# Fifth passes over 64 rows, two at a time, in the layer part of a language model's tower

## The reference

```python
def _block(x, g, bt, Wi, bi, cw, cb, wd, bd_, wB, bB_, wC, bC_, wo, bo):
    h = _layernorm(x, g, bt)
    uv = h @ Wi.T + bi
    u, v = (uv[..., :D], uv[..., D:])
    uc = _dwconv_causal(u, cw, cb)
    delta = jax.nn.softplus(uc @ wd.T + bd_)
    Bm = uc @ wB.T + bB_
    Cm = uc @ wC.T + bC_
    y = _selective_scan(uc, delta, Bm, Cm)
    y = y * jax.nn.sigmoid(v)
    return x + (y @ wo.T + bo)
```

## Time and profile before

| | |
|---|---|
| median of 3 executions | 1590.33 us (1590.24 to 1594.37) |
| profiled execution, own time | 1598.23 us |
| its span, first to last instruction | 1596.3 us |
| mean granted TensorE clock | 0.977 |
| TensorE matmul busy, share of span | 1506.3 us, 94% |
| TensorE weight load busy | 1232.6 us, 77% |
| VectorE busy | 1349.4 us, 85% |
| ScalarE busy | 1241.8 us, 78% |
| GpSimd busy | 836.2 us, 52% |

### The profile page before, as it was taken

One profiled execution on the slowest core, in us unless ns is written; L12 is line 12 of the kernel. 1 busy time (PEld: TensorE's weight loads), 2 busy tenths in 40 slices (PEclk: granted clock), 3 DMA queues, 4 the chain that ended last, 5 costly groups with the idle time before them and its releaser, 6 DMA issues.

```text
span 1596.3 us, 36428 instructions
## 1 busy us (share of the span) xinstructions
PE 1506.3 (94%) x11313; PEld 1232.6 (77%) x11313; DVE 1349.4 (85%) x3201; ACT 1241.8 (78%) x2686; POOL 836.2 (52%) x1428
## 2 busy tenths in 40 slices
PE   2699999999999999999999998999999999999986
PEld 1588878888888888888888886677777777777763
DVE  4699999999999999999999886678888878888763
ACT  2688878888888888888888963777787877877762
POOL 7777755443334453333333236566666666666642
PEclk9799999999999999999999997999999999999996
DMA  5311100000000000000000000000000000000000
GB/s 111 80 29 30 30 23 34 1 34 0 0 1 1 1 1 0 0 1 1 1 1 0 1 1 1 2 8 12 12 10 15 11 11 10 10 10 15 11 12 25
DMA packets 16571, 22.41 MB, mean 14 GB/s; under 512 B 2912, under 2 KB 13792, under 8 KB 16480
## 3 DMA queue, kind: packets, MB, share of 16 engines
q1 hardware_dynamic: 13408, 14.98, 2.8%
q0 software_dynamic: 3072, 6.30, 2.6%
HBM read 14.58 MB, written 6.29 MB: 13 GB/s over the span
## 4 chain that ended last, share of the span: by engine, by line
PE 60%; DVE 18%; ACT 9%; issue 9%; POOL 2%; DMA 1%; DVEq 1%; ACTq 0%; POOLq 0%
PE banks L706 9%; PE banks L921 7%; PE banks L697 7%; PE banks L889 6%; PE banks L846 5%; PE banks L873 5%; PE banks L860 4%; DVE hs_h L1500 3%; DVE x L1537 3%; DVE xs L1448 2%; PE banks L787 2%; PE banks L717 2%; PE banks L832 2%; PE banks L945 2%; PE banks L835 2%
## 5 line engine op out<-in xcount | busy, mean ns | idle before, releaser
L1593 DVE TENSOR_REDUCE mx<-banks 128x4 f32<-128x1024 f32 x192 | 234.2, 1220 | 45.6 <-PE banks L860 45.1
L1224 ACT ACTIVATE probs<-banks 128x1024 f32<-128x1024 f32 x192 | 195.7, 1019 | 84.5 <-PE banks L873 81.1
L503 POOL TENSOR_TENSOR x<-x,bo_row 128x768 f32<-128x768 f32 (+1 forms) x64 | 118.3, 1848 | 159.0 <-DVE ucr_r L1474 159.0
L697 PE MATMUL banks<-ht,w_uv 128*128 128x512 f32 x576 | 166.3, 398 | 14.3 <-ACT sv_l L1199 12.5
L479 POOL TENSOR_TENSOR lnt<-mv,const 128x4 f32<-128x4 f32 x64 | 20.4, 319 | 269.1 <-DVE mv L1439 268.8
L1465 DVE SCALAR_TENSOR_TENSOR uc_h<-u_h,vec,uc_h 128x512 f32<-128x512 f32 x192 | 146.9, 765 | 0.9 <-ACT uc_h L1137 0.9
L697 PEld LDWEIGHTS banks<-ht,w_uv 128*128 128x128 f32 x576 | 108.4, 191 | 42.0 <-issue 18.1
L1448 DVE SCALAR_TENSOR_TENSOR xs<-x,rstd,xs 128x192 fp32r<-128x192 f32 x256 | 89.9, 413 | 46.5 <-ACT xs L1176 46.5
L697 PE MATMUL banks<-ht,w_uv_rest 128*128 128x512 f32 x384 | 120.0, 394 | 0.0
L1116 ACT ACTIVATE u_l<-banks,vec 64x256 f32<-64x256 f32 x128 | 60.0, 469 | 73.5 <-PE banks L697 72.7
L873 PE MATMUL banks<-q_t,k_t 64*128 64x256 f32 x768 | 108.8, 334 | 7.7 <-ACT probs L1224 6.3
(11 more groups left out here) (191 smaller groups left out, 4662.8 us busy)
## 6 DMA issues: line engine op xcount, KB each, us to landing
out_dram<-y_out SPq DMA_DIRECT2D x32, 192.0 KB, 2.0
raw_z<-w_z_dram SPq DMA_DIRECT2D x4, 704.0 KB, 5.3
raw_uv<-w_uv_dram SPq DMA_DIRECT2D x4, 576.0 KB, 3.9
emb<-embedding_dram,idx POOLq DMA_INDIRECT x64
q_t<-mx_t SPq DMA_DIRECT2D x64, 6.0 KB
emb<-w_qkv_dram SPq DMA_DIRECT2D x1, 864.0 KB
w_o<-w_o_dram SPq DMA_DIRECT2D x1, 768.0 KB
bo_row<-bout_dram SPq DMA_DIRECT2D x4, 96.0 KB
```

The lines of the kernel that those rows point to most:

```text
L503: nc.gpsimd.tensor_tensor(rows, rows, bo_row[:, l, :][:, None, :].broadcast_to([P, CT, D]), ALU.add).then_inc(x_biased, 1)
L697: last = nc.tensor.matmul(out[:], w, r[:], start=(k == 0), stop=(k == len(passes) - 1))
L1224: act.activation(probs[:, (s + g // 2) % 2, g % 2, :].rearrange("p (j k) -> p j k", j=2), B_SST, ACT.Exp, scale=float(DH) ** -0.5).then_in ...
L1593: nc.vector.tensor_reduce(mx[:, s].rearrange("p t (j h) -> p j t h", j=2)[:, :, :, g], B_SS.rearrange("p j (t k) -> p j t k", t=2), AX, AL ...
```

## The change

The fifth pass of each product contracts only over the 64 rows that carry rounded low rows. Where it covered 128 rows (the other 64 being rest times rest, or zero weights), it now covers 64, and two such passes on different halves of the partitions are issued one behind the other. For Z, B and C the first sequence's pass uses rows 0 to 63 and the second's rows 64 to 127, each over 256 columns. For U low and V the pass covers all 512 columns; V's uses the rows 64 to 127, for which ScalarE copies the rounded low rows of `ht[1]` into a new tile `ht_low` (`low_again`, at the end of its step), and the weight rest of V is stored on the upper half. U high's pass has no partner of its own; Z's first pair follows it. TensorE waits for the copy before the first of the UV pair, and for its own earlier passes (semaphores z_low and bc_low) before it adds to banks that two row halves write.

```diff
+            def uv_passes(l, col, out, first):
...
                 passes = ((w_uv[:, s, 0, c], ht[0]), (w_uv[:, s, 1, c], ht[1]), (w_uv[:, s, 2, c], ht[2]),
-                          (w_uv_rest[:, s, 0, c], ht[0]), (w_uv_rest[:, s, 1, c], ht[1]))
+                          (w_uv_rest[:, s, 0, c], ht[0]))
...
+            def uv_low(l, col, b, out, first):
...
+                return nc.tensor.matmul(out[:], w_uv_rest[half(b), l % 2, 1, col:col + HI],
+                                        (ht_low if b else ht[1])[half(b), :], start=first, stop=not first,
+                                        skip_group_check=True)
...
+            def full_passes(l, col, s, q, out, first, last):
...
+                passes = ((w_z[:, w_s, 0, c], ucr_h), (w_z[:, w_s, 1, c], ucr_l), (w_z[:, w_s, 0, c], ucr_r),
+                          (w_z_rest[:, w_s, 0, c], ucr_h))
...
+            def low_pass(l, col, s, b, out, first, last):
...
+                return nc.tensor.matmul(out, w_z_rest[half(b), w_s, 1, c], ucr_l[half(b), s, b * S:(b + 1) * S],
+                                        start=first, stop=last, skip_group_check=True)
...
-                uv_product(l, UV_L, B_UVL).then_inc(ul_done, 1)
+                uv_passes(l, UV_L, B_UVL, True)
                 wait(pe, sv_ready, n)
-                uv_product(l, UV_V, B_VH).then_inc(uv_done, 1)
+                wait(pe, ht_low_ready, n + 1)
+                uv_low(l, UV_L, 0, B_UVL, False).then_inc(ul_done, 1)
+                uv_low(l, UV_V, 1, B_VH, True)
+                uv_passes(l, UV_V, B_VH, False).then_inc(uv_done, 1)
                 wait(pe, x_updated, n - 2)
-                uv_product(l, UV_H, B_UH).then_inc(uh_done, 1)
+                uv_passes(l, UV_H, B_UH, True)
+                uv_low(l, UV_H, 0, B_UH, False).then_inc(uh_done, 1)
...
-                z_product(l, Z_H, s, B_ZH).then_inc(zh_done, 1)
                 wait(pe, decay_ready, n)
...
-                z_product(l, Z_LC, s, B_ZCL).then_inc(z_done, 1)
+                low_pass(l, Z_H, s, 0, seq_of(B_ZH, 0), True, False).then_inc(z_low, 1)
+                low_pass(l, Z_LC, s, 1, seq_of(B_ZCL, 1), True, False).then_inc(z_low, 1)
+                full_passes(l, Z_H, s, BOTH, B_ZH[:], False, False)
+
+                wait(pe, z_low, 2 * (n + 1))
+                low_pass(l, Z_H, s, 1, seq_of(B_ZH, 1), False, True).then_inc(zh_done, 1)
+                low_pass(l, Z_LC, s, 0, seq_of(B_ZCL, 0), False, False)
+                full_passes(l, Z_LC, s, BOTH, B_ZCL[:], False, True).then_inc(z_done, 1)
...
-                z_product(l, B_H, s, B_BH)
-                b_low_product(l, s, B_BL).then_inc(b_done, 1)
-                z_product(l, C_H, s, B_CH).then_inc(c_done, 1)
+
+
+                low_pass(l, B_H, s, 0, seq_of(B_BH, 0), True, False).then_inc(bc_low, 1)
+                low_pass(l, C_H, s, 1, seq_of(B_CH, 1), True, False).then_inc(bc_low, 1)
+                full_passes(l, B_H, s, BOTH, B_BH[:], False, False)
+                wait(pe, bc_low, 3 * n + 2)
+                low_pass(l, B_LOW[0], s, 0, B_BL[:, 0:S], True, False).then_inc(bc_low, 1)
+                low_pass(l, B_H, s, 1, seq_of(B_BH, 1), False, True)
+                for b in range(2):
+                    full_passes(l, B_LOW[b], s, slice(b * S, (b + 1) * S), B_BL[:, 0:S], False, False)
+                wait(pe, bc_low, 3 * (n + 1))
+                low_pass(l, C_H, s, 0, seq_of(B_CH, 0), False, False)
+                low_pass(l, B_LOW[1], s, 1, B_BL[:, 0:S], False, True).then_inc(b_done, 1)
+                full_passes(l, C_H, s, BOTH, B_CH[:], False, True).then_inc(c_done, 1)
...
+            def low_again(it):
+                if it is None:
+                    return
+                n, l, c, s = it
+                wait(act, ht_ready, n + 1)
+                wait(act, uv_done, n)
+                act.activation(ht_low[half(1), :], ht[1][half(0), :].bitcast(F32), ACT.Identity).then_inc(ht_low_ready, 1)
...
                 gates(at(2))
+                low_again(at(1))
```

On GpSimd, and on VectorE for the first layer, the second of the two operations that make `w_uv_rest` becomes two over 64 rows each:

```diff
-                for k in range(2):
-                    nc.gpsimd.tensor_tensor(w_uv_rest[:, s, k, :], raw_uv[:, k, :], w_uv[:, s, k, :].bitcast(F32),
-                                            ALU.subtract).then_inc(w_split, 1)
+
+                for k, rows_, at_ in ((0, slice(0, P), 0), (1, half(0), 1), (2, half(1), 1)):
+                    if k > 0:
+
+                        pool.wait_ge(w_split, 5 * l + k)
+                    nc.gpsimd.tensor_tensor(w_uv_rest[rows_, s, at_, :], raw_uv[rows_, k, :],
+                                            w_uv[rows_, s, k, :].bitcast(F32), ALU.subtract).then_inc(w_split, 1)
```

More of the change, by code:

```diff
@@ L116, in build @@
         ht = [sa(f"ht_{k}", [P, 2 * S], F32R) for k in range(3)]
+        ht_low = sa("ht_low", [P, 2 * S], F32R)
         w_z = sa("w_z", [P, 2, 2, Z_COLS], F32R)
@@ L225, in build @@
         ht_ready = sem("ht_ready")
+        ht_low_ready = sem("ht_low_ready")
         uh_done = sem("uh_done")
@@ L236, in build @@
         sv_ready = sem("sv_ready")
+        z_low = sem("z_low")
+        bc_low = sem("bc_low")
         zh_done = sem("zh_done")
@@ L353, in layer_loads @@
             def layer_loads(l):
-                wait(sp, w_split, 4 * l)
+                wait(sp, w_split, 5 * l)
                 sp.dma_start(raw_uv[:], w_uv_d[:, l]).then_inc(s_layer[l], 16)
@@ L689, in means_of_sums @@
                 last.then_inc(means_done, 1)
-            def uv_product(l, col, out):
+            def uv_passes(l, col, out, first):
                 c, s = slice(col, col + HI), l % 2
                 passes = ((w_uv[:, s, 0, c], ht[0]), (w_uv[:, s, 1, c], ht[1]), (w_uv[:, s, 2, c], ht[2]),
-                          (w_uv_rest[:, s, 0, c], ht[0]), (w_uv_rest[:, s, 1, c], ht[1]))
+                          (w_uv_rest[:, s, 0, c], ht[0]))
                 for k, (w, r) in enumerate(passes):
-                    last = nc.tensor.matmul(out[:], w, r[:], start=(k == 0), stop=(k == len(passes) - 1))
-                return last
@@ L700, in z_product @@
[L700 to L704, removed]
-                for k, (w, r) in enumerate(passes):
[L706 to L719, removed]
+                    last = nc.tensor.matmul(out[:], w, r[:], start=first and k == 0, stop=not first and k == 3,
+                                            skip_group_check=True)
@@ new lines, in uv_passes @@
+                return last
+            def uv_low(l, col, b, out, first):
+                return nc.tensor.matmul(out[:], w_uv_rest[half(b), l % 2, 1, col:col + HI],
+                                        (ht_low if b else ht[1])[half(b), :], start=first, stop=not first,
+                                        skip_group_check=True)
+            def full_passes(l, col, s, q, out, first, last):
+                c, w_s = slice(col, col + HI), l % 2
+                passes = ((w_z[:, w_s, 0, c], ucr_h), (w_z[:, w_s, 1, c], ucr_l), (w_z[:, w_s, 0, c], ucr_r),
+                          (w_z_rest[:, w_s, 0, c], ucr_h))
+                for k, (w, r) in enumerate(passes):
+                    done = nc.tensor.matmul(out, w, r[:, s, q], start=first and k == 0,
+                                            stop=last and k == len(passes) - 1, skip_group_check=True)
+                return done
@@ L1378, in split_weights @@
                 dve.wait_ge(w_rounded, 5)
-                for k in range(2):
-                    nc.vector.tensor_tensor(w_uv_rest[:, 0, k, :], raw_uv[:, k, :], w_uv[:, 0, k, :].bitcast(F32),
-                                            ALU.subtract).then_inc(w_split, 1)
+                for k, rows_, at_ in ((0, slice(0, P), 0), (1, half(0), 1), (2, half(1), 1)):
+                    nc.vector.tensor_tensor(w_uv_rest[rows_, 0, at_, :], raw_uv[rows_, k, :],
+                                            w_uv[rows_, 0, k, :].bitcast(F32), ALU.subtract).then_inc(w_split, 1)
                 for k in range(2):
```

7 lines of the change are left out of this document (6 added, 1 removed).

## The result

| | before | changed |
|---|---|---|
| median, us | 1590.28 | 1667.39 |
| range of 4 executions | 1589.91 to 1594.37 | 1660.09 to 1668.38 |
| ratio, 95% interval | | 1.0458 [1.0434, 1.0482] |
| profiled execution, own time / span | 1598.23 / 1596.3 | 1668.12 / 1665.2 |

The change makes the kernel slower by 4.6% by the table's ratio. That ratio is not the quotient of the table's two medians, which would be 1.0485. The medians lie 77 us apart, the two profiled executions 69.9 us, and against 52 later executions of the kernel before (median 1592.8 us) the changed kernel's median is 74.6 us up, 4.7%. Forecast were 1650 us and 59 us more.

A forecast was written before the change was run, and what follows sets the result against it. TensorE was taken to set the pace at 13.72 us a step; +1.16 us a step, mostly changes of rows, summed with smaller terms to +59 us, from the median of 1590.3 to 1650 us, range 1622 to 1684.

The forecast's parts named there:

- What bounds: Layer part: TensorE sets the pace in 34 of 59 steps, 13.72 us each, and nearly does in the rest.
- The price of a change of rows: TensorE, long matmuls: each change between 128 and 64 rows costs 0.195 us, ends 0.18 and 0.22.
- The sum of a step: TensorE per step: 1.85 us removed, 1.06 of columns and 1.95 for ten changes of rows added; net +1.16, step 14.88.
- The copy is covered: ScalarE's ht_low copy ends 0.4 us before TensorE needs it; cost nothing, bounds 0 to 0.2 us a step.
- The sum over the kernel: Whole kernel: 39.4 + 5.0 + 10 + 2 + 2.3 us over the groups of steps, together +59.
- Rival 1: ScalarE's copy comes 0.2 to 0.4 us a step late beyond its cover: +17 us, 1667 us; chance 0.12.
- Rival 2: Changes of rows behind full 512-column matmuls are free: TensorE's step 12.93 us, time 1567 to 1590 us; chance 0.07.
- Rival 3: The two 64-row passes of a pair do not run side by side: 1.9 us a step, 1692 us; chance 0.03.
- The signs named beforehand: Profile after: 14.9 us steps, ScalarE idle 1.5 us or more before u_l, ht_low 0.6 us, VectorE's share down a twelfth.
- The chances of slower: Whole kernel: the forecast with rivals 1 and 3 given 0.91 for slower, same 0.03, faster 0.06.

The follow-up runs named there:

- e7: e2 with a single pass a step (Z high of the second sequence, 256 columns) over 64 rows, alone: 1613.61 us, ratio 1.0127.
- e3: The kernel before with the change made in B and C alone, three pairs in two new islands, no copy: 1613.75 us, ratio 1.0136.
- e1: The changed kernel with every low pass over 128 rows again, same order, waits and copy kept: 1611.86 us, ratio 1.0121.
- e2: e1 without ScalarE's copy and without TensorE's wait for it: 1598.12 us, ratio 1.0035.
- e4: e3 with its three pairs in one piece behind the output product's 64-row matmuls, no change of rows added: 1600.16 us, ratio 1.0042.
- e8: The changed kernel with ScalarE's copy moved forward, directly behind the operations that write ht: 1666.76 us, ratio 1.0470.
- e12: The kernel before with two B and C pairs around the output product's last 64-row matmuls and ScalarE's cb_l moved behind its xs: 1585.26 us, ratio 0.9953.
- e9: The kernel before with the fifth passes of Z, B and C left out, result a little less exact: 1594.13 us, ratio 1.0008.
- e10: The kernel before with ScalarE's cb_l moved behind its xs, alone: 1586.99 us, ratio 0.9970.

## Why the prediction was right, point by point

- **What bounds.** Right. TensorE set the pace in 34 of 59 steps, and its longer program made them longer: 13.72 to 15.08. In the other direction it did not hold: the loop between ScalarE and VectorE lies 0.08 us under it.
- **The price of a change of rows, 0.195 us.** Right, and shown three ways: e7 (0.20), the spacing in the changed kernel's trace, and e3, whose step was forecast from it at 14.27. The order and TensorE's waits on its own passes are ruled out by e1 and e2, 64 rows as such by e4. The reading behind it holds too: the 512-column pass at 497.39 streams 0.21 us by the prediction's figure for its columns, and the pair's weights come at 497.72, 0.11 later (0.10 in the prediction).
- **The sum of a step, +1.16 us.** Mis-sized; it measured +1.36. Two terms were off. The first pair of B and C was priced at its columns, 0.12; it follows one-column matmuls, which leave nothing to load weights behind, and cost 0.23: the weight load that began at 496.27 lies bare. And full passes of 512 columns follow each other by 0.227 in a long unbroken run, which the step before had over 25 passes; in the shorter runs between islands it is 0.231, times 20, another 0.09. With both, 13.72 + 1.16 + 0.11 + 0.09 = 15.08. These two terms were read from the changed kernel's trace after the result; only the first was tried again (e3).
- **The copy is covered.** Right in the changed kernel (0.6 us of cover in the trace, e8 no difference), and right that only TensorE's slowness covers it: e1 against e2 shows the price without cover, 0.30 us a step, above the bound of 0.2.
- **The sum over the kernel.** 34 steps 46 us instead of 39.4; the eight paced by VectorE 6.7 instead of 5.0; the 17 mixed ones 12.2 instead of 10; the first four 3.7 instead of 2; from the last group of transposes on 0 instead of 2.3. Together 69 instead of 59. The remaining 7 us of the 17 between 1650 and 1667 come from taking the profiled execution of before to the median: it stood 7.9 above its median, that of the changed kernel 0.7 above. The record shows what goes with this. An execution's time follows its mean granted clock: the kernel before took 1598.2 us at 0.977 (the profiled one), and later 1598.7 at 0.976 and 1587.3 at 0.987; the changed kernel took 1668.1 at 0.978 (the profiled one) and 1660.1 at 0.988. At like clocks the two kernels lie 70 to 73 us apart. The prediction took the 7.9 off on both sides, though three of the changed kernel's four executions ran at 0.978 to 0.980, about the clock of the profiled execution of before.
- **Rival 1, a late copy:** the loop exists, but not at this pace; it is e1's 14.07.
- **Rival 2, changes of rows free behind long passes:** fallen with e7. Its time was mis-sized too. Had it been true, 12.93 us on TensorE would have been worth nothing like 0.57: the loop between ScalarE and VectorE ends at 13.64, and with the copy in place e1's loop at 14.07, so by these two loops (argued, not run) the changed kernel would not have gained even then. TensorEngine Tiling (Array Packing) of the Trainium skill, Key Properties, has the rule that held, the drain at a change of tiling mode. Theoretical Speedup gives up to twice the rate for 64 rows or fewer; the halves did run side by side here, and the kernel still became slower, since an island costs 0.39 us beside its columns.
- **Rival 3, pairs that run one behind the other:** fallen; both start at 501.54.
- **The signs named beforehand:** a pair's full matmul follows 0.31 us after it (0.3 named), the copy takes 0.63 us and ends before TensorE asks for it, and VectorE's busy share falls from 93% to 85%. One failed: ScalarE stands idle 1.14 us before u_l, not 1.5 or more. Its further waits are 0.35 us at u_h and 0.44 at dc_l. The chances of slower add up to 0.90, not 0.91.
- Not tried: the copy removed from the changed kernel itself, since V's low pass needs it.

## What to carry to other kernels

Matmuls over half the rows, two side by side, save their columns once but pay for the way in and out: in these runs 0.39 us for an island, against 0.12 us saved by a pair over 256 columns. Put them where the array already works on 64 rows, and there behind matmuls with many columns (in e12 a pair cost 0.12 us behind 192 columns and 0.22 behind one column), or leave them. And before taking work off the engine that sets the pace, look for the loop just under it: leave the work out altogether once (e9) and see what the step falls by; here it was 0.05 us. Compare the steps and not the whole times alone, and look at the granted clock of both executions first: the times of the kernel before moved with it by 11 us, more than the 0.3% to 0.5% gained by e10 and e12.

## What the hardware showed that I had not expected

U high's low pass and Z's first pair stand in a row in the program: rows 0 to 63, rows 0 to 63, rows 64 to 127. In the changed kernel's timeline (PE rows) they are:

```profile
504.01 0.49 PE L714 MATMUL banks<-ht,w_uv_rest 64*128 64x512 f32 x1
504.02 0.60 PE L733 MATMUL banks<-ucr_l,w_z_rest 64*128 64x256 f32 x2
...
504.35 0.28 PE L733 MATMUL banks<-ucr_l,w_z_rest 64*128 64x256 f32 x1
```

The second row holds both of Z's passes, the last one shows the later of the two by itself. One of Z's two passes starts 0.01 us after U high's and the other 0.33 later, when U high's 512 columns are through. By the rows they use, the early one must be the third in the program (rows 64 to 127), started ahead of the second. That is an inference from the halves; the rows do not name them. It saved nothing, since the second had to wait in any case. Also new to me: full passes of 512 columns ran at 0.227 us in a run of 25 and at 0.231 in runs of four to eight, and no run here says why.
